# Image columns 4 to 6 of each cell added by accumulating transfers from GpSimd, in place of VectorE's pair sum

## Chip, cores and metric

One core of a Trainium2 chip. The metric is the device time of one launch in microseconds. The core's engines are TensorE (PE in the profile), VectorE (DVE), ScalarE (ACT), GpSimd (POOL) and SyncE (SP); each runs its own instructions in the order in which they are written and waits on semaphores. "POOLq" or "SPq" marks what an engine's queue issues, such as transfers.

## What is computed

A two-layer vision tower over 128 images. The part that the change touches is the first stage, a depthwise 3x3 convolution with a mean over cells of 8x8 pixels:

```python
B, H, W, C = ...            # 128 images, 64, 64, 128
y = lax.conv_general_dilated(x, conv_w, window_strides=(1, 1), padding=[(1, 1), (1, 1)],
      dimension_numbers=('NHWC', 'HWIO', 'NHWC'), feature_group_count=C) + conv_b
y = lax.reduce_window(y, 0.0, lax.add, (1, 8, 8, 1), (1, 8, 8, 1), 'VALID') / 64
ct = y.reshape(b, -1, C)     # 64 tokens of 128 features per image
h = ct
h = h + attention(layernorm(h));  h = h + experts(layernorm(h))        # layer 0: 2 shared, 8 routed
h = h + sparse_attention(layernorm(h));  h = h + triangular_mlp(layernorm(h))   # layer 1
```

Because the mean is linear, a cell's mean of the convolution needs only sums of pixels: over a cell's 8 columns it needs column 0 alone, column 7 alone, and the sum of columns 1 to 6, each summed over rows.

## The kernel before, in words

The 128 images are taken in 16 groups of 8. Four stages work on four groups at once, as a pipeline over 19 passes: in one pass `tok` (the convolution and pooling) works on group i, `att` (first attention) on the group before it, `ffn` (experts) on the one before that and `sec` (second layer) on the one before that. Image work stands in passes 0 to 15; from pass 2 on there is expert work beside it.

The order of the pieces in a pass is written out by hand for each engine in the table `ORDER` (line 51). A word such as `pool.1.0` or `hidden.14` is one piece; a mark ' means that it belongs to the pass before. Nothing reorders them afterwards: an engine that waits in one piece holds all that stands behind it.

The image of a group is read in 4 units u of two images, each in 2 halves v of 32 image columns. Half v always lands in buffer `xbuf[v]`, which holds 128 partitions (image, row) by 32 columns by 128 channels, 16 KB a partition, seen as `blocks[v]` with 4 cells of 8 columns. So a half-unit is one of eight (u, v) of a pass. Its way before the change:

- SyncE (L361) loads 2048 KB as one transfer, as soon as TensorE has read the buffer's last content (semaphore `pooled`).
- VectorE, piece `pair.u.v` (L878), adds columns 2, 4, 6 onto 1, 3, 5 in one instruction.
- GpSimd, pieces `add.u.0` and `add.u.1` for v = 0, `add.u.2` and `add.u.3` for v = 1 (L1133), adds columns 3 and then 5 onto column 1.
- ScalarE, piece `inner.u.v` (L663), writes the rounded bf16 half of column 1 over column 4; VectorE, same name (L882), writes the rest beside it.
- TensorE, pieces `pool.u.0` to `pool.u.3` (L410, L413, L418), sums over rows: `pool.u.0` and `pool.u.1` read buffer 0, `pool.u.2` and `pool.u.3` buffer 1. After them SyncE may load that buffer again.

GpSimd has other pieces between: `att.0`, `pre.1`, `att.9`, `post.2` are the power of the layer norms (L1114), whose result VectorE needs to normalise (L870); `pre.3` and `pre.4` add up the rotated q and the keys of the second layer (L1157, L1162), and VectorE's products for the keys (L1035, `pre.4`) may overwrite the q products only after `pre.3`; `pre.6`, `pre.7`, `score.2`, `score.4` are products of keys and head masks (L1175) that the scores (L560, L564) read; `hidden.q` for every fifth chunk q makes `hid_l` (L1141), which `down.q` on TensorE (L505 to L507) needs; `sum.q` adds to `moe` (L1148); `att.11` takes the gate's exponent (L1123), read by VectorE at L956. GpSimd also issues the 20 weight loads of the first passes (L1110, 128 rows of 2 KB each).

## Time and profile before

| | |
|---|---|
| median of 3 runs | 2192.52 us (2187.37 to 2193.03) |
| profiled execution | 2185.65 us, its span 2183.9 us |
| busy, share of the span | TensorE 86%, VectorE 86%, ScalarE 61%, GpSimd 55% |
| mean granted TensorE clock | 0.956 of 2.4 GHz |
| image loads | 128 of 2048 KB, 32.1% of the 16 transfer engines' time |

The span is the time from the first to the last instruction; the time of the launch is 1.75 us more. A busy TensorE is not TensorE at its peak: matmuls overlap, and the 512-column bf16 matmuls that read 0.38 us each start 0.216 us apart at the full clock. Timeline rows give the start, the duration (of several instructions together, where xN stands at the end) and, in brackets, how long the engine sat idle before and what released it.

### The profile page before, as it was taken

The page shows a single profiled execution, that of the slowest core. Times are in us where ns is not written, and L with a number is a line of the kernel's source. Part 1 is how long each engine was busy: PE and PEld are TensorE (multiplying, and loading weights), DVE is VectorE, ACT ScalarE, POOL GpSimd, SP SyncE. Part 2 cuts the span into 40 slices and gives each one's busy share as a digit, 9 for nine tenths or more (in the row PEclk, how much of TensorE's full clock was granted, in tenths as well). Part 3 has the DMA queues.
Part 4 walks back from the last instruction along what each step waited for, and adds up shares of the span by engine and source line. Part 5 has one row for each costly group of instructions (what it writes and reads, how often), then busy time and mean ns, then how long its engine had stood idle before and what let it go on. Part 6 is the DMA issues. An engine that isn't in the chain of part 4 may idle for free.

```text
span 2183.9 us, 38353 instructions
## 1 busy us (share of the span) xinstructions
PE 1868.5 (86%) x12224; PEld 1066.0 (49%) x12224; DVE 1880.1 (86%) x3524; ACT 1331.7 (61%) x2319; POOL 1207.4 (55%) x796
## 2 busy tenths in 40 slices
PE   2355889898988989798998989888998989899986
PEld 2344545455454545455454555545454555544444
DVE  1667899999999999899998989989998989987762
ACT  0234767666675766567675757657675756768752
POOL 1244557574755657575663757466565647554532
PEclk9999999999999999899998989999998989999996
DMA  5664534243343434334333424333343433200000
GB/s 181 250 241 183 193 123 155 114 159 151 121 160 117 155 121 155 122 145 165 121 129 137 155 94 160 150 122 150 125 155 112 164 122 124 109 6 1 5 6 5
DMA packets 33616, 282.00 MB, mean 129 GB/s; under 512 B 5470, under 2 KB 15649, under 8 KB 17020
## 3 DMA queue, kind: packets, MB, share of 16 engines
q1 hardware_dynamic: 18432, 268.44, 32.1%
q10 hardware_dynamic: 13372, 5.66, 0.9%
q0 software_dynamic: 1600, 5.24, 0.6%
q8 instruction: 112, 1.84, 0.3%
q14 instruction: 100, 0.82, 0.1%
HBM read 275.14 MB, written 4.19 MB: 128 GB/s over the span
## 4 chain that ended last, share of the span: by engine, by line
PE 40%; DVE 35%; issue 16%; DMA 2%; POOL 2%; ACT 2%; ACTq 1%; DVEq 1%; POOLq 0%
DVE taps L899 7%; DVE hid_l L991 7%; DVE xbuf L878 5%; PE pool_bank L413 4%; PE hid_bank L490 3%; PE down_bank L505 3%; PE hid_bank L492 3%; PE hid_bank L491 3%; PE down_bank L507 2%; PE down_bank L506 2%; PE sec_bank L528 2%; PE pool_bank L418 2%; PE sec_bank L544 2%; DMA xbuf<-in_x 2%; DVE k L870 2%
## 5 line engine op out<-in xcount | busy, mean ns | idle before, releaser
L732 ACT ACTIVATE hid_h<-hid_bank,b_s 128x512 bf16<-128x512 f32 x640 | 439.3, 686 | 280.9 <-PE hid_bank L492 221.9
L991 DVE TENSOR_TENSOR hid_l<-hid,hid_h 128x512 bf16<-128x512 f32 x512 | 498.3, 988 | 21.3 <-ACT hid L732 20.9
L1133 POOL TENSOR_TENSOR xbuf<-xbuf 128x512 f32<-128x512 f32 x256 | 359.8, 1405 | 266.1 <-DVE xbuf L878 257.2
L732 ACT ACTIVATE hid<-hid_bank,b_s 128x512 f32<-128x512 f32 x640 | 437.3, 683 | 0.0
L1141 POOL TENSOR_TENSOR hid_l<-hid,hid_h 128x512 bf16<-128x512 f32 x128 | 201.1, 1571 | 201.7 <-ACT hid L732 201.7
L1148 POOL TENSOR_TENSOR moe<-moe,part 128x512 f32<-128x512 f32 x128 | 196.6, 1536 | 179.9 <-DVE part L1008 178.1
L490 PE MATMUL hid_bank<-x2h,w1h 128*128 128x512 bf16 x640 | 253.8, 396 | 28.6 <-issue 17.7
L505 PE MATMUL down_bank<-hid_h,w2h 128*128 128x512 bf16 x640 | 252.5, 395 | 27.2 <-DVE part L1008 20.4
L899 DVE SCALAR_TENSOR_TENSOR taps<-pooled_s,tapw,taps 128x256 f32<-128x256 f32 (+1 forms) x416 | 269.6, 648 | 3.5
L878 DVE TENSOR_TENSOR xbuf<-xbuf 128x1536 f32<-128x1536 f32 x128 | 229.8, 1795 | 32.0 <-DMA xbuf<-in_x 23.6
L491 PE MATMUL hid_bank<-x2h,w1l 128*128 128x512 bf16 x640 | 250.9, 392 | 0.0
L492 PE MATMUL hid_bank<-x2l,w1h 128*128 128x512 bf16 x640 | 250.5, 391 | 0.0
L506 PE MATMUL down_bank<-hid_h,w2l 128*128 128x512 bf16 x640 | 250.4, 391 | 0.0
L507 PE MATMUL down_bank<-hid_l,w2h 128*128 128x512 bf16 x640 | 249.8, 390 | 0.0
L1175 POOL TENSOR_TENSOR keys_h<-keys,heads 128x632 f32<-128x632 f32 x128 | 206.9, 1640 | 4.7 <-PE sec_bank L564 3.4
L410 PE MATMUL pool_bank<-block_b,xbuf 128*128 128x48 bf16 x1024 | 50.5, 191 | 133.7 <-DVE xbuf L882 92.4
L413 PE MATMUL pool_bank<-block_sum,xbuf 128*128 128x48 f32 x1024 | 161.9, 308 | 0.0
L676 ACT ACTIVATE pooled_s<-pool_bank 128x384 f32<-128x384 f32 x192 | 90.4, 491 | 115.0 <-PE pool_bank L413 110.4
L1114 POOL TENSOR_TENSOR rs<-ve,power 128x4 f32<-128x4 f32 x64 | 80.8, 1262 | 139.0 <-DVE ve L865 136.4
L418 PEld LDWEIGHTS pool_bank<-block_sum,xbuf 128*128 128x128 f32 x1024 | 143.9, 211 | 11.2 <-issue 1.0
L413 PEld LDWEIGHTS pool_bank<-block_sum,xbuf 128*128 128x128 f32 x1024 | 148.1, 223 | 0.0
L418 PE MATMUL pool_bank<-block_sum,xbuf 128*128 128x48 f32 x1024 | 142.4, 288 | 0.0
(180 smaller groups left out, 3329.3 us busy)
## 6 DMA issues: line engine op xcount, KB each, us to landing
xbuf<-in_x SPq DMA_DIRECT2D x128, 2048.0 KB, 7.3
out<-h ACTq DMA_DIRECT2D x16, 256.0 KB, 2.2
hid<-in_w POOLq DMA_DIRECT2D x10, 256.0 KB, 4.4
part<-in_w POOLq DMA_DIRECT2D x10, 256.0 KB, 6.4
keys_h<-in_limit_c ACTq DMA_DIRECT2D x1, 167.5 KB
tw_s<-in_tw ACTq DMA_DIRECT2D x2, 64.0 KB
share_b<-in_pick_c ACTq DMA_DIRECT2D x1, 96.0 KB
ident<-in_ident_c ACTq DMA_DIRECT2D x1, 64.0 KB, 12.2
```

What stands on the lines that cost most here:

```text
L413: mm = nc.tensor.matmul(view[:, 1, :, side[bx]], blocks[v][:, bx, 0, :], block_sum[:], start=True, stop=True)
L418: mm = nc.tensor.matmul(view[:, :, v, side[bx]], blocks[v][:, bx, 7, :], block_sum[:], start=True, stop=True)
L490: nc.tensor.matmul(bank[:], w1h[:, e, cols], x2h[b][:], start=True, stop=False)
L491: nc.tensor.matmul(bank[:], w1l[:, e, cols], x2h[b][:], start=False, stop=False)
L492: nc.tensor.matmul(bank[:], w1h[:, e, cols], x2l[b][:], start=False, stop=True).then_inc(hid_done, 1)
L505: nc.tensor.matmul(down_bank[:], w2h[:, e, cols], hid_h[:, r, :], start=begin, stop=False)
L506: nc.tensor.matmul(down_bank[:], w2l[:, e, cols], hid_h[:, r, :], start=False, stop=False)
L732: nc.scalar.activation(dst[:, r, :], hid_bank[n % 2][:], ACT.Gelu, bias=b1_s[:, q:q + 1]) \
L878: nc.vector.tensor_tensor(v[:, :, 1:6:2, :], v[:, :, 1:6:2, :], v[:, :, 2:7:2, :], ALU.add) \
L899: nc.vector.scalar_tensor_tensor(dst, src, w, dst, ALU.mult, ALU.add).then_inc(tapped, 1)
L991: nc.vector.tensor_tensor(hid_l[:, q % RING, :], hid[:, q % HIDS, :], hid_h[:, q % RING, :], ALU.subtract).then_inc(hid_rest, 1)
L1133: nc.gpsimd.tensor_tensor(v[:, :, 1, :], v[:, :, 1, :], v[:, :, 2 * k + 3, :], ALU.add) \
```

## The change

SyncE no longer brings columns 4 to 6 of a cell. It issues two transfers for a half-unit, columns 0 to 3 (pieces of 2 KB, 4 a partition) and column 7 (pieces of 512 bytes, 4 a partition), 1280 KB together, and each raises `x_in` by 16. A new piece on GpSimd, `fold.u.v`, waits for both and issues a transfer of columns 4 to 6 (768 KB in HBM, pieces of 1536 bytes) that adds onto columns 1 to 3 in SBUF. It raises the new semaphore `x_added`. GpSimd's two additions wait for that instead of for VectorE, and add columns 2 and 3 onto column 1. VectorE's `pair` pieces and the semaphore `x_paired` are gone. TensorE's and ScalarE's order is the same; VectorE's is the same less the eight `pair` pieces; GpSimd's has eight `fold` pieces more.

```diff
-        x_in = [sem(f"x_in{i}", 16 * T) for i in range(2)]
-        x_paired, x_summed = sem("x_paired", 2 * T), sem("x_summed", 4 * T)
+        x_in = [sem(f"x_in{i}", 32 * T) for i in range(2)]
+        x_added = [sem(f"x_added{i}", 16 * T) for i in range(2)]
+        x_summed = sem("x_summed", 4 * T)
...
+        def cells_of(g, u, v):
+            src = x[bass.ds(g * GI + 2 * u, 2), :, v * (HW // 2):(v + 1) * (HW // 2), :]
+            return src.rearrange("i y (b x) c -> (i y) b x c", x=BX)
...
             def load(g, u, v):
-                src = x[bass.ds(g * GI + 2 * u, 2), :, v * (HW // 2):(v + 1) * (HW // 2), :]
-                eng.dma_start(xbuf[v][:], src.rearrange("i y x c -> (i y) x c")).then_inc(x_in[v], 16)
+                src = cells_of(g, u, v)
+                eng.dma_start(blocks[v][:, :, 0:4, :], src[:, :, 0:4, :]).then_inc(x_in[v], 16)
+                eng.dma_start(blocks[v][:, :, 7, :], src[:, :, 7, :]).then_inc(x_in[v], 16)
...
             def tokens(g, b, kind, u=0, k=0):
-                if kind == "pair":
-
-                    v = blocks[k]
-                    eng.wait_ge(x_in[k], at(x_in[k], g, 16 * (u + 1)))
-                    nc.vector.tensor_tensor(v[:, :, 1:6:2, :], v[:, :, 1:6:2, :], v[:, :, 2:7:2, :], ALU.add) \
-                      .then_inc(x_paired, 1)
-                elif kind == "inner":
+                if kind == "inner":
...
             def tokens(g, b, kind, u=0, k=0):
+                if kind == "fold":
+
+                    eng.wait_ge(x_in[k], at(x_in[k], g, 32 * (u + 1)))
+                    eng.dma_start(blocks[k][:, :, 1:4, :], cells_of(g, u, k)[:, :, 4:7, :], accum_op=ALU.add) \
+                       .then_inc(x_added[k], 16)
+                    return
                 half, k = k // 2, k % 2
                 v = blocks[half]
                 if k == 0:
-                    eng.wait_ge(x_paired, at(x_paired, g, 2 * u + half + 1))
+                    eng.wait_ge(x_added[half], at(x_added[half], g, 16 * (u + 1)))
                 else:
                     eng.wait_ge(x_summed, at(x_summed, g, 4 * u + 2 * half + 1))
-                nc.gpsimd.tensor_tensor(v[:, :, 1, :], v[:, :, 1, :], v[:, :, 2 * k + 3, :], ALU.add) \
+                nc.gpsimd.tensor_tensor(v[:, :, 1, :], v[:, :, 1, :], v[:, :, k + 2, :], ALU.add) \
                   .then_inc(x_summed, 1)
```

Where the folds stand on GpSimd is the second half of the change. The first place is in a full pass, from `hidden.4` to the start of unit 1. The kernel before has there, on GpSimd, hid_l of chunk 4, the two additions of half-unit (0, 1), the power of the third layer norm, and the first addition of half-unit (1, 0):

```order
L1141 TENSOR_TENSOR hid_l<-hid,hid_h 128x512 [waits hid_made]
L1130 REGISTER_ALU
L1133 TENSOR_TENSOR xbuf<-xbuf 128x4x128 [waits x_paired]
L1132 REGISTER_ALU
L1133 TENSOR_TENSOR xbuf<-xbuf 128x4x128 [waits x_summed]
L1113 ISA
L1114 TENSOR_TENSOR rs<-ve,power 128x4 [waits mom3]
L1130 REGISTER_ALU
L1133 TENSOR_TENSOR xbuf<-xbuf 128x4x128 [waits x_paired]
```

The changed kernel has in the same place:

```order
L1147 TENSOR_TENSOR hid_l<-hid,hid_h 128x512 [waits hid_made]
L1129 REGISTER_ALU
L1130 ISA [waits x_in0]
L1130 DMA xbuf<-in_x 128x4x384
L1139 TENSOR_TENSOR xbuf<-xbuf 128x4x128 [waits x_added1]
L1138 REGISTER_ALU
L1139 TENSOR_TENSOR xbuf<-xbuf 128x4x128 [waits x_summed]
L1113 ISA
L1114 TENSOR_TENSOR rs<-ve,power 128x4 [waits mom3]
L1130 ISA [waits x_in1]
L1130 DMA xbuf<-in_x 128x4x384
```

`fold.1.0`, which waits for buffer 0 of unit 1 (`x_in0`), now stands ahead of the additions of half-unit (0, 1), and `fold.1.1` behind the power of the layer norm. The other folds stand likewise: 2.0 ahead of `add.1.2`, 2.1 ahead of `add.2.0`, 3.0 ahead of `add.2.2`, 3.1 ahead of `add.3.0`; 0.0 at the start of the pass and 0.1 ahead of `add.0.0`.

The second place is on VectorE, in the same stretch. Before it has there, from its half of `inner.0.0` (L882), two hid_l and the pair sum of half-unit (0, 1):

```order
L882 TENSOR_TENSOR xbuf<-xbuf 128x4x128 [waits inner_high]
L990 REGISTER_ALU
L991 TENSOR_TENSOR hid_l<-hid,hid_h 128x512 [waits hid_made]
L990 REGISTER_ALU
L991 TENSOR_TENSOR hid_l<-hid,hid_h 128x512 [waits hid_made]
L878 TENSOR_TENSOR xbuf<-xbuf 128x4x3x128 [waits x_in1]
L1021 TENSOR_TENSOR h<-sec_bank,h_0 128x512 [waits moe_turned]
```

The changed kernel has there:

```order
L882 TENSOR_TENSOR xbuf<-xbuf 128x4x128 [waits inner_high]
L990 REGISTER_ALU
L991 TENSOR_TENSOR hid_l<-hid,hid_h 128x512 [waits hid_made]
L990 REGISTER_ALU
L991 TENSOR_TENSOR hid_l<-hid,hid_h 128x512 [waits hid_made]
L1021 TENSOR_TENSOR h<-sec_bank,h_0 128x512 [waits moe_turned]
```

Only the pair sum left; the seven other places on VectorE look alike.

## Rows read from the trace of the kernel before

**Rows 1.** Windows, 620 to 724 us: PE, PEld, DVE, ACT, POOL busy; clock, DMA

```profile
620.00:724.00 104.00, 93.07 (x599) 51.48 (x597) 94.69 (x180) 62.17 (x109) 61.70 (x40) 0.93 0.33 125
```

**Rows 2.** Page, part 4: shares of the chain that ended last, by line

```profile
DVE taps L899 7%; DVE hid_l L991 7%; DVE xbuf L878 5%; PE pool_bank L413 4%; PE hid_bank L490 3%; PE down_bank L505 3%; PE hid_bank L492 3%; PE hid_bank L491 3%; PE down_bank L507 2%; PE down_bank L506 2%; PE sec_bank L528 2%; PE pool_bank L418 2%; PE sec_bank L544 2%; DMA xbuf<-in_x 2%; DVE k L870 2%
```

**Rows 3.** One line, VectorE's pair sum: ns min/median/max, first and last start us

```profile
L878 DVE TENSOR_TENSOR xbuf<-xbuf x128: 1743/1750/2195, 16.3 to 1888.6; 128x1536 f32<-128x1536 f32 x128
```

**Rows 4.** Timeline, SyncE's queue: start us, duration us, engine, line, operation, count

```profile
686.75 11.11 SPq L361 DMA_DIRECT2D xbuf<-in_x  x2
...
711.80 16.89 SPq L361 DMA_DIRECT2D xbuf<-in_x  x2
...
739.98 12.60 SPq L361 DMA_DIRECT2D xbuf<-in_x  x2
```

**Rows 5.** DMA view: issuing queue, count, KB each, median us to landing

```profile
xbuf<-in_x SPq DMA_DIRECT2D x128, 2048.0 KB, 7.3
out<-h ACTq DMA_DIRECT2D x16, 256.0 KB, 2.2
hid<-in_w POOLq DMA_DIRECT2D x10, 256.0 KB, 4.4
part<-in_w POOLq DMA_DIRECT2D x10, 256.0 KB, 6.4
```

**Rows 6.** One line, GpSimd's weight loads: ns min/median/max, first and last start

```profile
L1110 POOL DMA_DIRECT2D hid<-in_w x10: 536/548/749, 92.4 to 171.7; - x10
```

**Rows 7.** Timeline, first place: GpSimd, VectorE and TensorE around the third layer norm

```profile
688.19 2.62 POOL L1133 TENSOR_TENSOR xbuf<-xbuf 128x512 f32<-128x512 f32 x2
...
690.90 1.40 POOL L1114 TENSOR_TENSOR rs<-ve,power 128x4 f32<-128x4 f32 x1
...
692.34 1.12 DVE L870 TENSOR_SCALAR x<-h,mv,rs 128x128 f32<-128x128 f32 x4 [0.31 <-POOL rs L1114]
...
694.82 0.60 PE L382 MATMUL sec_bank<-ident,x 128*128 128x128 f32 x4
```

**Rows 8.** Timeline, second place: GpSimd, VectorE and TensorE around the rotated keys

```profile
702.98 1.27 POOL L1157 TENSOR_TENSOR q<-keys_h 128x512 f32<-128x512 f32 x1 [3.86 <-DVE keys_h L1035]
...
704.72 0.68 DVE L1035 TENSOR_TENSOR keys_h<-sec_bank,cos 128x512 f32<-128x512 f32 x1
...
705.82 0.38 PE L533 MATMUL sec_bank<-xc,second_kc 128*128 128x120 f32 x2
```

**Rows 9.** Timeline, third place: GpSimd's key products and TensorE's third score

```profile
713.73 3.35 POOL L1175 TENSOR_TENSOR keys_h<-keys,heads 128x632 f32<-128x632 f32 x2
...
719.39 0.30 PE L560 MATMUL sec_bank<-limit_b,place_b 67*128 67x320 bf16 x1
```

**Rows 10.** Timeline, fourth place: GpSimd's hid_l of chunk 19 and its matmul

```profile
730.71 1.20 POOL L1141 TENSOR_TENSOR hid_l<-hid,hid_h 128x512 bf16<-128x512 f32 x1
...
736.34 0.38 PE L505 MATMUL down_bank<-hid_h,w2h 128*128 128x512 bf16 x1
```

**Rows 11.** Tile xbuf, the two halves (ns min/median/max); timeline, the pooling matmul

```profile
L663 ACT ACTIVATE xbuf<-xbuf x128: 626/630/662, 32.1 to 1897.2; 128x512 bf16<-128x512 f32 x128
L882 DVE TENSOR_TENSOR xbuf<-xbuf x128: 676/686/1024, 32.8 to 1902.8; 128x512 bf16<-128x512 f32 x128
...
750.80 0.36 PE L410 MATMUL pool_bank<-block_b,xbuf 128*128 128x48 bf16 x8
```

**Rows 12.** Timeline, sixth place: GpSimd's exponent of the gate and its reader on VectorE

```profile
760.87 5.82 POOL L1123 TENSOR_TENSOR ez<-euler,lg 128x32 f32<-128x32 f32 x1 [5.39 <-DVE lg L950]
...
770.31 0.18 DVE L956 TENSOR_REDUCE esum<-ez 128x4 f32<-128x32 f32 x1
```

**Rows 13.** Timeline, SyncE's queue in the first two groups

```profile
37.60 4.29 SPq L361 DMA_DIRECT2D xbuf<-in_x  x2
...
180.93 0.33 SPq L361 DMA_DIRECT2D xbuf<-in_x  x1
```

More of the change, by code:

```diff
@@ L43 @@
 STAGES = ("tok", "att", "ffn", "sec")
-STAGE_OF = dict(pair="tok", add="tok", inner="tok", pool="tok", tap="tok", out="tok",
+STAGE_OF = dict(fold="tok", add="tok", inner="tok", pool="tok", tap="tok", out="tok",
                 att="att", low="att", up="ffn", hidden="ffn", down="ffn", sum="ffn", pre="sec",
@@ new lines @@
+        weights.18 pool.3.2 pool.3.3 hidden.33 hidden.34 hidden.35 post.3 att.13 hidden.36 hidden.37 post.4
+        weights.19 hidden.38 hidden.39 post.5 out""",
+    dve="""
+        hidden.38' att.0 hidden.0 weights.0 sum.39' hidden.1 att.1 inner.0.0 weights.1 hidden.2 hidden.3
+        weights.2 pre.0 pre.1 hidden.5 hidden.6 pre.2 weights.3 hidden.7 inner.0.1 weights.4 pre.5 pre.3 sum.7
+        weights.5 hidden.8 pre.4 inner.1.0 hidden.10 att.4 weights.6 hidden.11 hidden.12 hidden.13 att.5 score.0
+        weights.7 score.1 sum.11 weights.8 score.2 inner.1.1 hidden.15 score.3 hidden.16 weights.9 hidden.17
+        hidden.18 weights.10 sum.15 tap.0.0 score.4 tap.0.1 score.5 tap.0.2 score.6 weights.11 tap.0.3 score.7
+        tap.0.4 inner.2.0 hidden.20 tap.0.5 sum.19 tap.0.6 att.7 tap.0.7 hidden.21 tap.0.8 weights.12 value.0
+        att.8 value.1 hidden.22 att.9 inner.2.1 value.2 hidden.23 att.10 value.3 tap.0.9 weights.13 sum.23
+        weights.14 tap.0.10 value.4 hidden.25 tap.0.11 hidden.26 value.5 att.11 weights.15 inner.3.0 value.6
+        weights.16 tap.0.12 hidden.27 value.7 hidden.28 tap.0.13 post.1 tap.0.14 post.2 sum.27 att.12 inner.3.1
@@ L86 @@
         weights.17 hidden.30 hidden.31 weights.18 tap.1.0 post.3 tap.1.1 tap.1.2 low tap.1.3 hidden.32 tap.1.4
-        tap.1.5 sum.31 tap.1.6 hidden.33 tap.1.7 tap.1.8 hidden.35 tap.1.9 hidden.36 tap.1.10 hidden.37
-        tap.1.11 sum.35 tap.1.12 tap.1.13 post.5 tap.1.14 weights.19""",
+        tap.1.5 sum.31 tap.1.6 hidden.33 tap.1.7 tap.1.8 hidden.35 tap.1.9 hidden.36 tap.1.10 hidden.37 tap.1.11
+        sum.35 tap.1.12 tap.1.13 post.5 tap.1.14 weights.19""",
     pool="""
-        sum.27' sum.31' weights.0 weights.1 weights.2 sum.35' weights.3 hidden.39' add.0.0 add.0.1 att.0
@@ L91 @@
-        weights.4 sum.39' hidden.4 add.0.2 add.0.3 pre.1 weights.5 weights.6 add.1.0 add.1.1 pre.3 hidden.9
-        weights.7 weights.8 pre.4 pre.6 weights.9 weights.10 add.1.2 pre.7 weights.11 add.1.3 hidden.14
-        score.2 weights.12 score.4 weights.13 add.2.0 weights.14 add.2.1 hidden.19 sum.7 sum.11 sum.15 sum.19
-        add.2.2 add.2.3 weights.15 att.9 hidden.24 add.3.0 add.3.1 weights.16 weights.17 att.11 add.3.2
-        weights.18 add.3.3 post.2 post.1 weights.19 hidden.29 sum.23 hidden.34""")
+        fold.0.0 sum.27' sum.31' weights.0 weights.1 weights.2 sum.35' weights.3 hidden.39' fold.0.1 add.0.0
@@ new lines @@
+        add.0.1 att.0 weights.4 sum.39' hidden.4 fold.1.0 add.0.2 add.0.3 pre.1 weights.5 weights.6 fold.1.1
+        add.1.0 add.1.1 pre.3 hidden.9 weights.7 weights.8 pre.4 pre.6 weights.9 weights.10 fold.2.0 add.1.2
+        pre.7 weights.11 add.1.3 hidden.14 score.2 weights.12 score.4 weights.13 fold.2.1 add.2.0 weights.14
+        add.2.1 hidden.19 sum.7 sum.11 sum.15 sum.19 fold.3.0 add.2.2 add.2.3 weights.15 att.9 hidden.24 fold.3.1
+        add.3.0 add.3.1 weights.16 weights.17 att.11 add.3.2 weights.18 add.3.3 post.2 post.1 weights.19
@@ L98, in read @@
+        hidden.29 sum.23 hidden.34""")
 def read(text):
@@ L392, in tokens @@
                     if k in (0, 2):
-                        eng.wait_ge(x_in[v], at(x_in[v], g, 16 * (u + 1)))
+                        eng.wait_ge(x_in[v], at(x_in[v], g, 32 * (u + 1)))
                     if k in (0, 3):
```

43 lines of the change are left out of this document (15 added, 28 removed).

## The prediction

> **What bounds the kernel now.** I read the table by windows first. In one stretch of the steady part, 104 us long, TensorE is busy for 93.07 us and VectorE for 94.69, GpSimd for only 61.70 [rows 1]: two engines share the bound. Next, the chain that ended last, by line: VectorE's pair sum L878 has 5% of it [rows 2], some 109 of 2183.9 us. Each of its 128 instructions takes 1750 ns [rows 3], 14.0 us in a pass over one group of 8 images. So the target is real. Last I read the queue that loads the image, because the change puts a new step behind each load. SyncE reissues a buffer's load as soon as TensorE has read it; the six loads of one pass that matter were issued at 686.75, 697.53, 711.80, 728.36, 739.98 and 752.25 us [rows 4] (a row there merges two issues; the second lasts 0.33 us and ends with the row).
>
> **What goes.** VectorE loses 14.0 us a pass. That pays only where the chain runs on VectorE. It does between the sixth load (752.25) and the first of the next pass, where three of the eight pair sums lie; I book 3 x 1.75 = 5 us a pass there. In the other five places the chain is worked out anew below, and their gain is in it.
>
> **What each load costs now.** A load of 2048 KB lands 7.3 us after issue and a transfer of 256 KB in 2.2 [rows 5]. On a straight line between these, the 1280 KB that SyncE still brings land in 5.1 us; with 0.3 us for its second issue, 5.4. I bound it by 5.1 and 7.6 (the old time plus that issue); it can't fall under the 2.2 us of the smallest. The fold then occupies GpSimd while it writes out its transfers. The nearest row is a weight load issued from GpSimd: 548 ns for 128 rows [rows 6]. A fold has 128 x 4 = 512 pieces. Bounds: 0.55 us (pieces cost nothing), 4.4 us (linear in pieces and doubled, since an addition also reads its target). I take the linear 2.2, because this work is a program's loop over pieces. With 0.3 us for hand-overs, GpSimd is free again **D = 5.4 + 2.2 + 0.3 = 7.9 us** after SyncE's issue, between 6 and 12.
>
> The Trainium skill speaks against my 2.2: its page "DMA: Bandwidth & Descriptors", section on the anatomy of a DMA issued from GpSimd, says one can emit a lot of descriptors before the incremental cost shows up. By that rule D would be 6.3 and the sum below 2325 us. No row here has more than 128 rows in one such issue, so the trace can't decide it.
>
> **Where it is paid.** GpSimd works in the order written. In six places of a pass the fold of the next half-unit stands ahead of the additions of the present one (the first order piece), and the load it waits for is issued only when TensorE has read that buffer, just before GpSimd arrives. Before, nothing on GpSimd waited for that load. So everything behind the fold is late. The time at which it now reaches TensorE, against when TensorE stood there:
>
> 1. Load 686.75, GpSimd free 694.65. Two additions 2.62, the layer norm's power 1.40, VectorE's normalisation 1.12 [rows 7]: 699.8. TensorE transposed that at 694.82 [rows 7]. **+5.0**
> 2. Load 697.53, free 705.4. Additions 2.7, sum for q 1.27, VectorE's next product 0.68 [rows 8]: 710.1. TensorE's matmul into that bank stood at 705.82 [rows 8]. **+4.3**
> 3. Load 711.80, free 719.7. One addition 1.3, two key products 3.35 [rows 9]: 724.4. The score matmul that needs them stood at 719.39 [rows 9]. **+5.0**
> 4. Load 728.36, free 736.3. Additions 2.7, hid_l 1.20 [rows 10]: 740.2. Its matmul stood at 736.34 [rows 10]. **+3.9**
> 5. Load 739.98, free 747.9. Additions 2.7, the split into halves on ScalarE 0.63 and VectorE 0.69 [rows 11]: 752.0. The pooling matmul stood at 750.80 [rows 11]. **+1.2**
> 6. Load 752.25, free 760.2. Additions 2.7, the gate's exponent 5.82 [rows 12]: 768.7; VectorE read it at 770.31 [rows 12]. **0**
>
> Together +19.4 us a pass. Each is a wait in TensorE's fixed order, and stretches 1 to 3 are ones in which TensorE itself is the chain. Less the 5 us: **+14.4**. Folds 1 and 2 of a pass stand where their data has long landed; they cost GpSimd 2.2 us each beside idle time. The later waits of the additions on the accumulation itself cost nothing if it lands within the some 15 us until its addition's turn; 256 KB from GpSimd land in 4.4 us [rows 5], and 768 KB I put at 6 to 10. ScalarE's work is unchanged.
>
> **The sum.** Full passes with image work: 16 groups less the first two, 14 x 14.4 = 202 us. The first two groups have little beside them; there the chain is the buffers themselves. From 37.60 to 180.93 us buffer 0 was freed seven times, 143.3 us in which the two buffers worked in parallel [rows 13]. Now one half-unit follows the other: D + additions 2.6 + halves 1.4 + matmuls and hand-overs 3.1 = 15 us, 14 of them 210 us: +67. The profiled execution took 2185.65 us, so 2185.65 + 202 + 67 = 2455; the median of the runs, 2192.5, lies 7 us above it, which I halve: **2458 us**, 12% slower.
>
> **Bounds.** At D = 6 the five delays fall to 10.6: 14 x 5.6 = 78, first groups +44: 2308. At D = 10 they are 29.9, and the sixth place starts to count, 30.4: 14 x 25.4 = 356, first groups +92: 2634. At D = 12: 2830. The price is about 69 us for each us of D.
>
> **Rivals.**
> - *The waits are half absorbed.* While TensorE waits, VectorE catches up with its backlog, so the VectorE-bound stretch afterwards shrinks by half of the 19.4. For it: VectorE is busy 94.69 of 104 us. Against: the stretch's work waits on TensorE's results in its own order. 2186 + 14 x (14.4 - 9.7) + 67 = 2319.
> - *The accumulation lands late.* It has its place at the additions: an addition's turn comes some 15 us after its fold, less GpSimd's time, so from a landing of about 13 us on it sets the pace at all eight half-units. At 20 us: 14 x 8 x 5 = 560 more than 2186, near 2800 with the first groups. For it: one of the two kinds of weight load from GpSimd, 256 KB each, took 6.4 us [rows 5], and three times that is 19. Against: the other kind took 4.4.
> - *Faster: the relief wins.* If GpSimd is free by 4.2 us after the load's issue, five delays shrink under what VectorE saves, and the sum crosses 2186; if they vanish, 2186 - 14 x 14.0 = 1990, and as TensorE is busy 93 of 104 us, about 2010. For it: the pair sum's 5% of the chain [rows 2]. Against: the line through both landings [rows 5] gives 5.1 us for the data alone.
> - *A lower clock.* The granted clock is already 0.93 in that stretch [rows 1], so about 15 of 104 us ran at the lower level, 1.2 GHz. Twice as much would add 7 us a pass, 98 in all: 2556, inside the range.
>
> The Trainium skill's page "SBUF — State Buffer", section on the two sides, gives another cause of delay: VectorE locks GpSimd out of a shared port, and descriptors aren't written meanwhile. Here the weight loads issued beside a busy VectorE took at most 749 ns against 536 [rows 6], so the trace allows some 0.2 us of it, and I add none.
>
> **Numbers.** Waits as worked out, D from 6 to 10: 0.62. Half absorbed: 0.14. Late accumulation or D above 10: 0.12. Faster: 0.09. No change: 0.03. A measurement of this kernel tells about 0.3% from no change. So slower by over 0.3% has 0.88, within it 0.03, faster 0.09. The range 2280 to 2650 holds the first case and most of the second, about 8 in 10.
>
> **What would show it.** In the new profile GpSimd's longest wait should be for the loads, at six places a pass and about 6 us each, not VectorE's pair sum. GpSimd's time for one fold should read 2.2 us (0.55 if the rule holds). TensorE should show new waits before the x3 transposes (L382), L533, L560 and L505 of 4 to 5 us, and SyncE's issues should be spaced 15 us or more in every place where they were spaced 10.8, 14.3, 16.6, 11.6 and 12.3. VectorE's busy time should fall by 230 us. The prediction is wrong if a load plus fold needs under 5 us, if the additions wait for the accumulation instead, or if TensorE doesn't wait at those places.

## The result and the profile after

The changed kernel takes **2897.1 us** (median of 4 runs, 2891.6 to 2908.4), the kernel before 2189.9 in the same session: a ratio of 1.324 (95% interval 1.321 to 1.327). The forecast was slower, but 2458 us, and its range ended at 2650. The profiled execution has a span of 2889.9 us at a granted clock of 0.838, against 2183.9 at 0.956.

The page of the changed kernel, part 1 (busy time of each engine) and part 4 (shares of the chain that ended last, by engine and by line; the line of before is in [rows 2]):

```profile
PE 2174.6 (75%) x12224; PEld 1221.4 (42%) x12224; DVE 1676.5 (58%) x3396; ACT 1332.8 (46%) x2319; POOL 1251.8 (43%) x924
...
PE 33%; DMA 20%; issue 16%; DVE 13%; POOL 12%; ACT 2%; SPq 2%; ACTq 1%; POOLq 0%; DVEq 0%
DMA xbuf<-in_x 20%; POOL xbuf L1139 8%; PE pool_bank L419 5%; PE pool_bank L424 3%; DVE taps L899 3%; PE hid_bank L496 3%; PE hid_bank L497 2%; PE hid_bank L498 2%; DVE x L876 2%; DVE cols L906 2%; PE down_bank L511 2%; PE down_bank L512 2%; PE down_bank L513 2%; SPq L366 1%; PE sec_bank L550 1%
```

The image loads, 2% of the chain before, are 20% of it now. The same 12224 matmuls take longer, and no engine is busy for more than 75% of the span.

Who waited for whom in the changed kernel: us in total, times, longest us.

```profile
POOL xbuf L1130 <- DMA xbuf<-in_x: 971.4, 99, 24.7
ACT xbuf L669 <- POOL xbuf L1139: 536.9, 98, 14.0
...
DVE xbuf L882 <- ACT xbuf L669: 300.5, 53, 25.9
```

The fold's line by itself (ns min/median/max, who waited for it, landing):

```profile
L1130 POOL DMA_DIRECT2D xbuf<-in_x x128: 1278/1319/1463, 8.3 to 2583.2; - x128
...
  POOL xbuf L1139: 13.3, 4
...
DMA to landing us min/median/max: 7.7/7.9/13.2
```

SyncE's two loads in the DMA view (KB each, median us to landing; the whole load is in [rows 5]):

```profile
xbuf<-in_x SPq DMA_DIRECT2D x128, 1024.0 KB, 5.8
...
xbuf<-in_x SPq DMA_DIRECT2D x128, 256.0 KB, 6.1
```

A fold lasts 1.32 us and lands in 7.9, and the additions waited for it only 4 times, 13.3 us in all. The waiting is for the loads ahead of it.

**Where the time is.** VectorE starts the expert sum once in a pass; the starts of the 15 waits ahead of it (L1000) give 14 intervals. I call the mean of the first twelve a steady pass. The windows from the first to the last start, before and then after (columns as in [rows 1]):

```profile
329.10:2038.10 1709.00, 1562.04 (x10442) 873.52 (x10440) 1582.24 (x2972) 1134.48 (x1976) 1022.18 (x649) 0.96 0.34 127
```

```profile
460.30:2744.20 2283.90, 1847.94 (x10442) 1019.97 (x10440) 1441.40 (x2869) 1134.39 (x1976) 1044.36 (x752) 0.82 0.45 95
```

A steady pass went from 124.8 to 170.1 us: 12 x 45.2 = 543. The thirteenth interval grew by 31.7, the start before the first mark by 131.2, together 706. VectorE's busy time fell by 10.1 us an interval, TensorE's rose by 20.4.

SyncE's issue times show where inside a pass. Before, a pass of the longer kind (they alternate between about 122 and 127 us), and after, the pass from 770.01:

```profile
808.67 11.10 SPq L361 DMA_DIRECT2D xbuf<-in_x  x2
...
833.71 0.33 SPq L361 DMA_DIRECT2D xbuf<-in_x  x1
...
936.01 0.33 SPq L361 DMA_DIRECT2D xbuf<-in_x  x1
```

```profile
770.01 0.37 SPq L366 DMA_DIRECT2D xbuf<-in_x  x1
...
788.32 0.37 SPq L366 DMA_DIRECT2D xbuf<-in_x  x1
...
812.04 0.37 SPq L366 DMA_DIRECT2D xbuf<-in_x  x1
```

| from load to load | before | after | more | more, mean of 12 passes | forecast |
|---|---|---|---|---|---|
| 1.0 to 1.1 (place 1) | 10.8 | 18.3 | 7.5 | 7.4 | 5.0 |
| 1.1 to 2.0 (place 2) | 14.3 | 23.7 | 9.4 | 8.7 | 4.3 |
| 2.0 to 2.1 (place 3) | 16.6 | 21.3 | 4.7 | 6.8 | 5.0 |
| 2.1 to 3.0 (place 4) | 11.6 | 18.3 | 6.7 | 6.5 | 3.9 |
| 3.0 to 3.1 (place 5) | 12.3 | 16.6 | 4.3 | 4.4 | 1.2 |
| 3.1 to 0.0 (place 6) | 20.0 | 29.2 | 9.2 | 7.7 | 0 |
| 0.0 to 0.1 | 8.3 | 7.6 | -0.7 | -1.3 | 0 |
| 0.1 to 1.0 | 33.5 | 38.5 | 5.0 | 4.7 | 0 |
| the relief, booked between 3.1 and 1.0 | | | | | -5.0 |
| sum | 127.4 | 173.5 | 46.1 | 45.1 | 14.4 |

(Loads are numbered u.v, half-unit by half-unit. The means are over the passes of the fourth to the fifteenth group.) The pass shown is unusual at place 3: the mean there is 23.4 us, not 21.3. From load 3.1 to the next 1.0, where the forecast booked a gain of 5 us, a mean pass lost 11.1.

### The profile page after: what moved, and what is told of

Same layout as the page of the kernel before. It is cut to its first block, busy times and chain, and to the rows that moved or that the text cites. A ratio compares the mean times of both kernels' runs of the same rounds, so it can differ in the third digit from the quotient of the medians.

```text
span 2889.9 us, 38831 instructions
## 1 busy us (share of the span) xinstructions
PE 2174.6 (75%) x12224; PEld 1221.4 (42%) x12224; DVE 1676.5 (58%) x3396; ACT 1332.8 (46%) x2319; POOL 1251.8 (43%) x924
## 4 chain that ended last, share of the span: by engine, by line
PE 33%; DMA 20%; issue 16%; DVE 13%; POOL 12%; ACT 2%; SPq 2%; ACTq 1%; POOLq 0%; DVEq 0%
DMA xbuf<-in_x 20%; POOL xbuf L1139 8%; PE pool_bank L419 5%; PE pool_bank L424 3%; DVE taps L899 3%; PE hid_bank L496 3%; PE hid_bank L497 2%; PE hid_bank L498 2%; DVE x L876 2%; DVE cols L906 2%; PE down_bank L511 2%; PE down_bank L512 2%; PE down_bank L513 2%; SPq L366 1%; PE sec_bank L550 1%
## 5 line engine op out<-in xcount | busy, mean ns | idle before, releaser
L1130 POOL DMA_DIRECT2D xbuf<-in_x x128 | 168.6, 1318 | 1003.4 <-DMA xbuf<-in_x 971.4
L991 DVE TENSOR_TENSOR hid_l<-hid,hid_h 128x512 bf16<-128x512 f32 x512 | 451.3, 895 | 136.5 <-ACT hid L738 135.6
L1139 POOL TENSOR_TENSOR xbuf<-xbuf 128x512 f32<-128x512 f32 x256 | 402.6, 1573 | 22.1 <-DMA xbuf<-in_x 13.3
L496 PE MATMUL hid_bank<-x2h,w1h 128*128 128x512 bf16 x640 | 288.5, 451 | 64.8 <-issue 28.9
L669 ACT ACTIVATE xbuf<-xbuf 128x512 bf16<-128x512 f32 x128 | 80.6, 630 | 536.9 <-POOL xbuf L1139 536.9
L882 DVE TENSOR_TENSOR xbuf<-xbuf 128x512 bf16<-128x512 f32 x128 | 151.0, 1180 | 300.5 <-ACT xbuf L669 300.5
L497 PE MATMUL hid_bank<-x2h,w1l 128*128 128x512 bf16 x640 | 286.4, 448 | 0.0
L1147 POOL TENSOR_TENSOR hid_l<-hid,hid_h 128x512 bf16<-128x512 f32 x128 | 166.6, 1302 | 220.7 <-ACT hid L738 220.7
L419 PE MATMUL pool_bank<-block_sum,xbuf 128*128 128x48 f32 x1024 | 189.0, 343 | 0.0
L424 PEld LDWEIGHTS pool_bank<-block_sum,xbuf 128*128 128x128 f32 x1024 | 170.0, 243 | 14.7 <-issue 3.0
L419 PEld LDWEIGHTS pool_bank<-block_sum,xbuf 128*128 128x128 f32 x1024 | 174.7, 257 | 0.0
L424 PE MATMUL pool_bank<-block_sum,xbuf 128*128 128x48 f32 x1024 | 165.8, 317 | 0.0
```

What stands on the lines that cost most here:

```text
L419: mm = nc.tensor.matmul(view[:, 1, :, side[bx]], blocks[v][:, bx, 0, :], block_sum[:], start=True, stop=True)
L424: mm = nc.tensor.matmul(view[:, :, v, side[bx]], blocks[v][:, bx, 7, :], block_sum[:], start=True, stop=True)
L496: nc.tensor.matmul(bank[:], w1h[:, e, cols], x2h[b][:], start=True, stop=False)
L497: nc.tensor.matmul(bank[:], w1l[:, e, cols], x2h[b][:], start=False, stop=False)
L991: nc.vector.tensor_tensor(hid_l[:, q % RING, :], hid[:, q % HIDS, :], hid_h[:, q % RING, :], ALU.subtract).then_inc(hid_rest, 1)
L1139: nc.gpsimd.tensor_tensor(v[:, :, 1, :], v[:, :, 1, :], v[:, :, k + 2, :], ALU.add) \
```

## The experiments

All times are medians, with the ratio to the kernel before run beside them; "pass" is the steady pass, 124.8 us before.

### Waiting alone, finer loads alone, the relief alone, late folds

**wait** puts into the kernel before nothing but GpSimd's waits, at the places of the folds:

```
+ if kind == "fold":
+     eng.wait_ge(x_in[k], at(x_in[k], g, 16 * (u + 1)))
+     return
```

> The kernel before, unchanged but for one thing: at the eight places where the change puts a fold, GpSimd now waits for that half-unit's load and issues nothing. Loads, pair sums and all arithmetic are the old ones. Theory A (GpSimd's wait in its fixed order is the whole cost, and my sum priced it too low): the old load lands 7.3 us after its issue, so GpSimd is free 7.6 us after it where the change has 7.9, and the time is near the changed kernel's, 2800 to 2950 us. Theory B (the waits cost the 14 x 14.4 + 67 us of my sum, and the rest is in the finer transfers, the accumulations and what they collide with): 2400 to 2500 us. Theory C (nearly all of it is in the transfers): under 2300 us.

Measured 2707.3 us, 1.235 (1.231 to 1.238), pass 157.0. Below theory A's range and far above B's and C's. **Waits that move no byte and add no instruction cost 515 us**, nearly double my whole forecast.

**split** loads in three transfers, pair sums kept:

```
- eng.dma_start(xbuf[v][:], ...)
+ eng.dma_start(blocks[v][:, :, 0:4, :], src[:, :, 0:4, :])
+ eng.dma_start(blocks[v][:, :, 4:7, :], src[:, :, 4:7, :])
+ eng.dma_start(blocks[v][:, :, 7, :], src[:, :, 7, :])
```

> The kernel before with each load in three transfers of the sizes that the change uses (columns 0 to 3, 4 to 6 and 7 of each cell, so rows of 2048, 1536 and 512 bytes), all issued by SyncE; VectorE's pair sum stays. Theory A: the second and third issue put the landing off by some 0.6 us and by nothing else, at two or three places where the load is on the path: 2190 to 2230 us. Theories B and C (finer transfers themselves cost): over 2300 us.

Measured 2224.9, 1.016 (1.014 to 1.018), pass 125.9: theory A.

**relief** is the changed kernel without folds:

```
- fold.0.0 ... fold.3.1 in GpSimd's order
- eng.wait_ge(x_added[half], at(x_added[half], g, 16 * (u + 1)))
+ eng.wait_ge(x_in[half], at(x_in[half], g, 32 * (u + 1)))
```

> The changed kernel without the folds and without their waits: an addition on GpSimd waits for its own load at its own place. Columns 4 to 6 of each cell are left out of the sum and aren't loaded. This is the relief alone: no pair sum on VectorE, loads of 1280 KB in two transfers. Theory A: under 2190 us by what VectorE's 14 us a pass are worth; by the 5 us that I booked 2120, if all of it pays 1994. Theory C: no faster than before, since the finer loads cost as much.

Measured 2146.9, 0.980 (0.977 to 0.982), pass 122.3. The pair sums are worth 2.6 us a pass beside the finer loads, 3.6 if a pass of split is the measure. Theory A's "under 2190" holds and C falls. I had booked 5, of the 14.0 that VectorE no longer works.

**late** keeps everything of the change and moves six folds on GpSimd to where, by the trace of the kernel before, their load has landed; one of them:

```
- hidden.4 fold.1.0 add.0.2 add.0.3 pre.1 weights.5 weights.6 fold.1.1 add.1.0
+ hidden.4 add.0.2 add.0.3 pre.1 fold.1.0 weights.5 weights.6 add.1.0
```

> The changed kernel, whole, with only GpSimd's order changed: in the six places where a fold waited, it stands later, where by the trace of the kernel before its load has landed (after the layer norm's power, after the sum for q, after the fourth addition and hid_l, between the sums of the experts, before the later powers). Each addition then waits for its accumulation, issue plus 14 to 15 us, where it came 9.7, 14.5, 15.6, 13.0, 12.4 and 14.4 us after the issue before. Theory A: most of the 707 us comes back, 2150 to 2350 us. Theory C: no more than 150 us of it comes back, over 2700 us.

Measured 2415.9, 1.104 (1.100 to 1.108), pass 137.7. 481 of the 707 us came back with the order alone, though 66 us fewer than theory A allowed. Its waits show what is late next:

```profile
POOL xbuf L1139 <- DMA xbuf<-in_x: 321.1, 89, 9.1
...
POOL xbuf L1130 <- DMA xbuf<-in_x: 215.1, 69, 19.1
```

The additions now wait for the accumulation: my rival of the late landing, which the change itself does not show. The second row says that the folds still wait for their loads too, 3.1 us in each of 69 places: late shortened the waits of the change and did not do away with them.

### Which places, and through which queue

**hold** is the changed kernel whose folds only wait (columns 4 to 6 are left out):

```
- eng.dma_start(blocks[k][:, :, 1:4, :], cells_of(g, u, k)[:, :, 4:7, :], accum_op=ALU.add) \
-    .then_inc(x_added[k], 16)
```

> The changed kernel with folds that only wait: the order, the places and the two loads of the change, but no accumulating transfer, so columns 4 to 6 are left out of the sum and aren't read. Its distance from the changed kernel (2897 us) is what the accumulations themselves cost; its distance from the relief alone (2147 us) is what the waits cost there. Theory A (the waits' cost is the same whatever the loads are): the added 515 us of the waits alone, less the 46 us of the relief alone, 2190 + 515 - 46, that is 2630 to 2690 us, which leaves some 240 us for the accumulations. Theory B (the accumulation costs nothing by itself; smaller loads only lengthen the wait): over 2800 us.

Measured 2596.1, 1.186 (1.182 to 1.190), pass 150.1: 34 us below theory A's range, and theory B falls. GpSimd is free about 6.7 us after the issue here and 7.6 in wait; against relief the waits cost 449 us, in wait 515. That is 66 us for some 0.9 us, **about 70 us for each us of D**. It is one comparison of two pairs that also differ in VectorE's pair sums, so it is an estimate. To the change, 301 us are left.

**five_waits** and **one_wait** are wait with the waits of places 1 to 5 only and of place 6 only:

```
- fold.0.0 fold.0.1 fold.3.1                                        (five_waits)
- fold.0.0 fold.0.1 fold.1.0 fold.1.1 fold.2.0 fold.2.1 fold.3.0    (one_wait)
```

> The kernel before with GpSimd's bare waits at places 1 to 5 of the prediction only (each wait for the load that SyncE issues just before). My prediction priced these at 19.4 us a pass, 272 in all, with GpSimd free 7.9 us after the issue; here it is 7.6. Theory A (the price of each place was about right, the rest is at places that I put at nothing): 2400 to 2500 us. Theory B (each wait costs more than the delay at TensorE's next use, since what runs after it is slowed too): over 2550 us.

> The kernel before with GpSimd's bare wait at place 6 of the prediction only, which I priced at 0. Theory A (place 6 was misjudged: the halves of the image come late on ScalarE, whose order has them ahead of the attention weights that TensorE waits for): some 6 us a pass, 2250 to 2300 us. Theory B (the place was priced right): 2185 to 2200 us.

Measured: 2635.1, 1.206 (1.197 to 1.214), pass 152.2 (+27.3); and 2281.0, 1.042 (1.039 to 1.045), pass 131.0 (+6.2). Together 532 us, and wait has 515: the places nearly add up. Theory B holds for the five, theory A for place 6: **the place priced at nothing costs 89 us**. TensorE's own waits in one_wait:

```profile
PE sec_bank L575 <- ACT p3t L760: 60.9, 15, 5.3
```

**one_wait_moved** moves the split that follows, on ScalarE and (likewise) on VectorE:

```
- turn.5 att.10 inner.3.0 turn.6 weights.15 hidden.27 turn.7
+ turn.5 att.10 turn.6 weights.15 hidden.27 turn.7 inner.3.0
```

> As the bare wait at place 6 alone, but with the split into halves that follows it moved behind three other pieces on ScalarE (turn.6, hidden.27, turn.7) and behind value.6, hidden.27 and value.7 on VectorE, so that these no longer stand behind the late additions. Theory A (it is the in-order queue of ScalarE, then VectorE, through which place 6 is paid): most of what the single wait cost is gone, 2185 to 2215 us. Theory B (it is paid otherwise, through what stands behind the wait on GpSimd itself, the gate's exponent, or through the late pooling): the same time as the single wait, within 10 us.

Measured 2223.3, 1.015 (1.011 to 1.019), pass 126.5. The wait above shrinks to:

```profile
PE sec_bank L575 <- ACT p3t L760: 1.0, 2, 0.7
```

So 58 of the 89 us went with the place of the split in ScalarE's and VectorE's orders (the time is 8 us above theory A's range); where the other 31 are paid stays open. The additions behind GpSimd's wait are late, `inner.3.0` waits for them, and behind it stands the copy that TensorE needs. I had looked only at what stands behind the fold on GpSimd.

**five_moved** does the same to the five other splits; one of them on VectorE:

```
- inner.1.0 hidden.10 att.4 pair.1.1 weights.6
+ hidden.10 att.4 pair.1.1 inner.1.0 weights.6
```

> The five bare waits (2635 us), with the splits into halves that follow each moved one to four pieces later on ScalarE and on VectorE, so that less stands behind the late additions there. Theory A (most of what the waits cost beyond my sum runs through these in-order queues): 2330 to 2480 us. Theory B (it runs through the other pieces behind the wait on GpSimd, the powers and the products for the keys, as my sum had it): 2560 us or more.

Measured **2719.2**, 1.241 (1.238 to 1.245), pass 157.9: 84 us slower than five_waits, where theory A had it 150 to 300 faster. Theory A falls. The time lies in theory B's open range, but B gives no reason for a loss. Waits in five_moved, and the same two in five_waits:

```profile
POOL xbuf L1137 <- DMA xbuf<-in_x: 833.5, 80, 24.2
...
PE pool_bank L411 <- DVE xbuf L883: 192.5, 71, 33.6
```

```profile
POOL xbuf L1137 <- DMA xbuf<-in_x: 765.0, 80, 24.2
...
PE pool_bank L411 <- DVE xbuf L883: 143.1, 25, 33.6
```

A later split means a later pooling on TensorE, so a later next load, so a longer next wait on GpSimd. (The moved orders without any wait were not run, here or for one_wait_moved, so what the order costs by itself is not shown.) **The loads form a ring.** The chain of waits of five_waits goes round it once in each place; from load 1.0 to load 1.1:

```profile
859.38 7.21 DMA xbuf<-in_x
...
866.75 1.26 POOL xbuf L1137
868.09 1.26 POOL xbuf L1137
869.35 0.98 POOL rs L1115
...
870.64 0.84 DVE x L871 x3
871.53 1.12 PE sec_bank L383 x4
872.64 1.57 PE pool_bank L419 x8
...
874.54 1.76 PE pool_bank L414 x8
876.46 7.27 DMA xbuf<-in_x
```

### The clock

In that chain four transposes take 1.12 us where [rows 7] have 0.60. TensorE had just waited for them (62.1 us in 15 times in all), and the granted clock from 871.5 to 876.4 us is 0.50, the lower level of 1.2 GHz. In one_wait the granted clock of the 6 us after the wait is 0.50 too. **filled** puts 24 matmuls with unused results ahead of that wait, **five_filled** 47 ahead of four of the five waits, **three_filled** those without the eight of one place. To stand ahead of the wait that matters, the fillers of the last two also swap the order of TensorE's waits at three places; the code below is that of filled.

```
+ for _ in range(24):
+     nc.tensor.matmul(b1[:, P:4 * P], w1h[:, 0, 0:P], w1h[:, 0, 0:3 * P], start=True, stop=True)
```

> The bare wait at place 6 alone (2281 us, 89 above before) with 24 more matmuls on TensorE just ahead of turn.6, into free columns of a PSUM bank, their result unused: about 4 us of work inside the wait of 4.6 us that the trace shows there. Theory A (half of the wait's price is the lower clock at which TensorE works after it: its busy time rose by 45 us): the filler keeps the clock up and the time falls to 2230 to 2250 us. Theory B (the clock after the wait isn't on the path): 2275 us or more.

> The five bare waits (2635 us) with 47 more matmuls of 512 columns a pass on TensorE, result unused, each lot just ahead of a place where it waits: 16 before the x3 transposes (wait 3.91 us), 8 before the product for the compressed keys (1.78), 9 before the third score (2.25), 14 before down.19 (3.46); 10 us of work at full clock inside 11.4 us of waits. Theory A (half of what the waits cost is TensorE's work after each of them at the lower clock): the granted clock rises and the pass falls from 147.3 to 136 to 141 us, the time to 2480 to 2550 us. Theory B (the lower clock is off the path, as it mostly was at place 6, since VectorE or GpSimd end last there): 2600 us or more.

> The five bare waits with the filling matmuls at three places only (16, 9 and 14), without the eight before the product for the compressed keys, which in the last run stood on the path for 2.8 us a pass. Theory A (the lower clock after the waits is a fifth or so of what they cost): 2560 to 2585 us, a steady pass near 146.5. Theory B (it is nothing, and what five_filled gained was chance): within 15 us of 2635. Theory C (it is half): under 2530.

Measured: filled 2273.7, 1.038 (1.035 to 1.041), pass 129.4; five_filled 2606.4, 1.193 (1.187 to 1.198), pass 149.2; three_filled 2605.3, 1.187 (1.181 to 1.193), pass 148.7. The windows after the wait, of one_wait and of filled:

```profile
792.00:798.00 6.00, 5.30 (x42) 2.99 (x43) 2.33 (x7) 4.12 (x8) 4.89 (x1) 0.50 0.00 1
```

```profile
786.00:792.00 6.00, 5.96 (x60) 3.62 (x59) 5.04 (x11) 4.98 (x9) 6.00 (x2) 1.00 0.02 4
```

The clock came back in full in filled, and from 0.87 to 0.93 over the steady stretch of five_filled, yet the passes gained only 1.6 and 3.0 to 3.5 us of the 6.2 and 27.3. Theory A of filled and of five_filled (half of the price) falls; B holds for five_filled and lies 1 us above filled's time. three_filled fits none of its three: 20 us above A (a fifth or so), 15 below B (nothing), and C (half) falls.

These gains are net. In filled the 24 matmuls stand before turn.6, while TensorE's wait of one_wait comes later, before turn.7. That wait shrank from 60.9 us in 15 times to 15.8 in 15, but the gate's product between the two (L460) came 3.9 us later behind turn.5 in the pass read, and what that cost is not known. In three_filled the stretches from load 1.0 to 3.1 are 5.6 us a pass shorter than in five_waits (means of twelve passes), a fifth of the price, and 2.4 of these are lost again between load 3.1 and the next 0.0. In five_filled the eight matmuls before the compressed keys put TensorE's product there 2.6 us later; leaving them out changed nothing in the whole. Where TensorE ran faster it waited longer for VectorE: in three_filled the wait before the compressed keys grew to

```profile
PE sec_bank L541 <- DVE keys_h L1045: 46.3, 13, 3.7
```

from 23.8 us in 13 times in five_waits.

### What the accumulation costs

**plain** writes where the change adds; **small** folds only the first of four cells:

```
- eng.dma_start(..., accum_op=ALU.add)
+ eng.dma_start(...)
```

```
- blocks[k][:, :, 1:4, :], cells_of(g, u, k)[:, :, 4:7, :]
+ blocks[k][:, 0:1, 1:4, :], cells_of(g, u, k)[:, 0:1, 4:7, :]
```

> The changed kernel with the same transfers from GpSimd, same size and pieces, but writing instead of adding, so the old contents of columns 1 to 3 are left out of the sum. Theory A (the 301 us that the accumulations add to the bare waits, 2897 against 2596, come from GpSimd's issue and from the transfers' volume, not from the addition): within 30 us of 2897. Theory B (the addition in the transfer engines is what costs): 2600 to 2800 us.

> The changed kernel with folds of a quarter: only the first of the four cells in each row is folded, so each accumulating transfer has 192 KB in 128 pieces of 1536 bytes where the change has 768 KB in 512, and columns 4 to 6 of the other cells are left out. Theory A (what the accumulation adds grows with its pieces and bytes): near a quarter of the 301 us over the bare waits, 2650 to 2700 us. Theory B (it is a fixed price per issue from GpSimd): over 2820 us.

Measured 2794.8, 1.274 (1.271 to 1.278), pass 163.9; and 2810.0, 1.282 (1.277 to 1.287), pass 164.7. The addition itself costs 102 us: by its number that is theory B, at the edge of its range. The fold's line in plain and in small:

```profile
L1130 POOL DMA_DIRECT2D xbuf<-in_x x128: 756/795/943, 8.2 to 2487.6; - x128
```

```profile
L1130 POOL DMA_DIRECT2D xbuf<-in_x x128: 864/893/1044, 8.2 to 2495.9; - x128
```

A plain issue of 512 pieces takes 0.80 us, an adding one of 128 pieces 0.89 and an adding one of 512 pieces 1.32. Of the 301 us, 214 stay at a quarter of the pieces and bytes: mostly a price per issue. Neither theory of small had that right; B, with over 2820, came nearer.

The landing does not carry the 102 us: the additions waited for it 13.3 us in all in the change and 2.9 in plain. The issue may. GpSimd's next instruction starts 0.82 us after a fold in both kernels, but in the change it then lasts longer. GpSimd's additions, in the change and in plain:

```profile
L1139 POOL TENSOR_TENSOR xbuf<-xbuf x256: 1252/1756/1830, 21.4 to 2593.9; 128x512 f32<-128x512 f32 x128
```

```profile
L1139 POOL TENSOR_TENSOR xbuf<-xbuf x256: 1252/1272/1819, 17.4 to 2500.4; 128x512 f32<-128x512 f32 x128
```

So the first addition behind a fold ends 9.87 us after the load's issue in the change, 9.37 in plain, 9.40 in small and 7.96 in hold (means over the six places). As an estimate, the cost over hold divided by the time of one issue is some 230, 250 and 240 us for each us in the change, plain and small: within a tenth, the three pay by how long the issue lasts. That the addition costs through the issue is thus likely and not shown apart.

**two_folds** folds only half-units 0.0 and 0.1, where nothing waits; **two_hold** takes those two transfers away again; **two_apart** and **late_apart** move the two folds to gaps in GpSimd's work:

```
- fold.0.0 sum.27' sum.31' ... hidden.39' fold.0.1 add.0.0 add.0.1 att.0 weights.4 sum.39'
+ sum.27' sum.31' fold.0.0 ... hidden.39' add.0.0 add.0.1 att.0 fold.0.1 weights.4 sum.39'
```

> The whole computation, with folds only at the first two half-units of a pass, where my prediction found their load long landed; the other six are loaded in one transfer and summed on VectorE as before. Theory A (a fold whose load has landed costs nothing, and VectorE's relief of two pair sums is worth a quarter of what eight are): 2175 to 2195 us, at best slightly under the kernel before. Theory B (accumulations cost wherever they stand, through the transfers): over 2220 us.

> The kernel with two folds (2253 us), whose folds now only wait and issue nothing; columns 4 to 6 of the first two half-units of each group are left out. Theory A (the 62 us are paid through the issue from GpSimd and what it holds up on VectorE): 2170 to 2200 us. Theory B (they come from the finer loads or the changed buffers' order): over 2230 us.

> The kernel with two folds (2253 us), whole, with these moved on GpSimd to where the trace shows it idle on both sides: fold.0.0 behind the second expert sum, fold.0.1 behind the first layer norm's power. Theory A (a VectorE instruction that starts beside a busy GpSimd lasts until GpSimd's unbroken run of work ends, so a fold that joins two runs costs VectorE more than one that stands alone): 2195 to 2225 us. Theory B (the issue costs the same wherever it stands): 2245 to 2260 us.

> The kernel with late folds (2416 us), whole, with fold.0.0 and fold.0.1 moved likewise. Theory A: 30 to 60 us less, 2355 to 2390 us. Theory B: within 10 us of 2416.

| | us | ratio (interval) | pass |
|---|---|---|---|
| two_folds | 2253.4 | 1.028 (1.025 to 1.030) | 129.2 |
| two_hold | 2197.2 | 1.004 (1.002 to 1.007) | 124.9 |
| two_apart | 2205.6 | 1.009 (1.006 to 1.012) | 126.0 |
| late_apart | 2363.1 | 1.081 (1.078 to 1.083) | 133.2 |

two_folds lies in theory B's range, but B's reason, the transfers, falls with two_apart, which keeps them. Theory A holds for the other three. Two folds that wait for nothing in a steady pass cost 4.4 us, and 3.2 of these go when they stand elsewhere. VectorE's rows in the changed kernel say how; then the two that answer to them in the kernel before:

```profile
908.95 1.37 POOL L1147 TENSOR_TENSOR hid_l<-hid,hid_h 128x512 bf16<-128x512 f32 x1 [10.05 <-ACT hid L738]
...
909.22 3.97 DVE L899 SCALAR_TENSOR_TENSOR taps<-pooled_s,tapw,taps 128x256 f32<-128x256 f32 x2
...
910.27 1.33 POOL L1130 DMA_DIRECT2D xbuf<-in_x  x1
...
911.12 1.77 POOL L1154 TENSOR_TENSOR moe<-moe,part 128x512 f32<-128x512 f32 x1
...
922.68 3.28 DVE L906 SCALAR_TENSOR_TENSOR cols<-pooled_s,tapw,taps 128x128 f32<-128x128 f32 x2
...
923.11 1.30 POOL L1130 DMA_DIRECT2D xbuf<-in_x  x1
923.94 3.65 POOL L1139 TENSOR_TENSOR xbuf<-xbuf 128x512 f32<-128x512 f32 x2
```

```profile
657.71 2.80 DVE L899 SCALAR_TENSOR_TENSOR taps<-pooled_s,tapw,taps 128x256 f32<-128x256 f32 x2
...
670.00 0.99 DVE L906 SCALAR_TENSOR_TENSOR cols<-pooled_s,tapw,taps 128x128 f32<-128x128 f32 x2
```

GpSimd's instruction behind a fold starts 0.8 us after it, before the issue has ended, and a VectorE instruction that starts beside the issue lasts until about the end of that next one: until 913.19, where GpSimd's ends at 912.89, and until 925.96, where the first of the two additions ends at 925.70. It is not held to the end of GpSimd's unbroken run, as theory A of two_apart has it: the second addition goes on to 927.60. Against the kernel before, VectorE's rows are 1.2 and 2.3 us longer. Over the 14 intervals VectorE was busy 25.9 us longer in two_folds than in two_hold, 1.9 us each. The rest of the 4.4 I can't assign; a candidate is the issue gap of TensorE before its `hid_bank` matmuls, 28.7 us in 5 times against 16.2. It wasn't tried apart.

## Why the prediction was wrong

**The sum of a steady pass.** The waits with the small loads (hold) +25.3; two folds that wait for nothing +4.4; the addition itself +6.1 (change against plain); 9.4 left of 45.2, in which GpSimd is free 8.2 us after the issue instead of 6.7, in six places. These are differences of whole kernels and overlap (the addition's 6.1 holds that of the two folds too), so the sum is a guide and no exact split. The relief is inside the 25.3. The waits are thus the greater part, and the forecast for a whole pass was 14.4.

- *What bounds the kernel.* Held in the main: of VectorE's 14 us a pass only 3.6 were worth anything, where I had booked 5. Its busy time fell by 204 us, not 230, as other instructions grew longer.
- *D = 7.9 us.* Held, partly by luck. From issue 812.04 to the addition at 819.94 are 7.90; over six places it is 8.2. The load's part was 7.1, not 5.4, the fold's 0.8, not 2.2. It lasts 1.32, but the next addition starts before its end and is then longer by 0.5 (1.76 against 1.27 in plain), so that in effect the fold took 1.3 and D was 8.7.
- *The 2.2 us of the fold.* The runs have 0.80 us for 512 plain pieces, against 0.55 for the 128 of a weight load [rows 6], and 1.32 for 512 adding ones, against 0.89 for 128. Both prices that the forecast named, 2.2 and 0.55, missed the 1.32. The rule of the Trainium skill's page "DMA: Bandwidth & Descriptors" (section on the anatomy of such a DMA) that I set against 2.2 comes nearer than the linear price: four times the pieces added 0.25 and 0.43 us. D did not fall to its 6.3, as the load took 1.7 us more than forecast.
- *The delay at TensorE's next use.* Held at the places named. After the issue of each load TensorE's instruction came at 13.4, 13.5, 12.2 and 12.6 us, before at 8.1, 8.3, 7.6 and 8.0 [rows 7 to 10]: +5.3, +5.2, +4.6 and +4.6, where the forecast had 5.0, 4.3, 5.0 and 3.9. Two of them in TensorE's rows:

```profile
783.39 0.90 PE L388 MATMUL sec_bank<-ident,x 128*128 128x128 f32 x3 [5.16 <-DVE x L876]
...
845.99 0.39 PE L511 MATMUL down_bank<-hid_h,w2h 128*128 128x512 bf16 x1 [4.28 <-POOL hid_l L1147]
```

- *The step that failed: that this delay is all.* From that instruction to the next load's issue took 4.9, 10.3, 9.1 and 5.7 us, before 2.7, 6.0, 9.0 and 3.6: another 8.7 us in this pass, 9.8 in the mean of twelve. The forecast had these stretches unchanged. They run in part at the lower clock and through VectorE, and as the loads form a ring, each us there is paid. The forecast's premise was that a load is issued "just before GpSimd arrives", and it expected waits of about 6 us. They last 9.8 in the mean, as GpSimd comes to the fold 2.6 us before the load is even issued, and at places 2, 3 and 4 it comes 4 to 6 us before.
- *Places 5 and 6, and the gain behind them.* The second failure, 1.2 and 0 against 4.3 and 9.2. It is the larger one: from load 3.1 to the next 1.0 a mean pass lost 11.1 us where I had booked a gain of 5, so 16 of the 30.8 us that the pass missed lie there. Some 6 of them go with the folds' transfers and their issues, since hold, without these, loses only 4.7 there. I followed what stands behind the fold on GpSimd and not what stands behind the late splits on ScalarE: TensorE waits for p3t, 2.50 and then 6.14 us:

```profile
881.13 1.08 PE L581 MATMUL sec_bank<-ident,e 128*80 128x128 f32 x4 [6.14 <-ACT p3t L766]
```

- *Folds 1 and 2 cost nothing.* Wrong: 4.4 us a pass. I had allowed 0.2 us for a delay of GpSimd's issue by VectorE and nothing for the reverse, which is what VectorE's rows show (3.28 us for 0.99). The Trainium skill's page "SBUF — State Buffer" (section on the two sides) calls the port pair that both share an exclusive lock, held for a whole instruction while the other engine is fully blocked. The trace agrees that VectorE is held; but where GpSimd's instructions overlap, it is held through several of them, not one.
- *First groups.* Right in kind: the third group's first load went out at 261.83 us, before at 180.93 [rows 13], +81 where I had 67 from 15 us a half-unit; from 42.04 us on it was 15.7.
- *The price of D.* The forecast says 69 us for each us of D, but its own bounds, 2308 at 6 and 2634 at 10, give 81. The runs gave about 70. In the bounds the first groups also move by 12 us for each us of D, where its sum has 14 half-units.
- *Rivals.* "Half absorbed" went the wrong way. "Lands late" fell in the change and is true of late. "Lower clock" was right in kind; the filled kernels got back 3.5 of the 27.3 us of five waits, half of the 7 it put on a pass (5.6 between load 1.0 and 3.1, less what was lost again behind).

A pass thus cost 45.2 us, not 14.4; 14 passes times the difference of 30.8 is 431 us, near the 439 between forecast and result. That is partly luck: the first groups cost 14 us more than forecast, and the thirteenth interval only 31.7, not 45.2. No version here beats the kernel before: the nearest whole one, two_apart, is 0.9% slower. The relief alone has 2% to give, and leaves columns out.

## What to carry to other kernels

- A wait put into an in-order queue is priced from the resource it waits for, round the whole ring back to that resource. If the awaited transfer can start only after work that stands behind the wait, or behind what this work feeds on any other engine, the two buffers work in series. Compare the spacing of the loads with latency plus everything between.
- Follow a late result through every in-order queue that consumes it, and price what stands behind each consumer. The cheapest cure was the order: the same transfers issued later gave back 481 of 707 us.
- Bare waits in the old kernel are a cheap first experiment: they gave 515 us without any of the new code.
